# A fused transformer layer on one core: the cross attention's norm and query projection move behind the first experts, its query's copies to the end of the queue

## What is computed

```
x = x + norm(attn_block(norm(x)))
x = x + norm(moe_block(norm(x)))
attn_block(h): q,k,v = ln1(h) @ c_attn        # 16 heads of 8, causal
               h = h + softmax(q k^T) v @ attn_proj
               q = lnx(h) @ q_attn            # k,v from the encoder states
               h = h + softmax(q k^T + scorer, masked) v @ x_proj
               return h + gelu(ln2(h) @ fc) @ mlp_proj
moe_block(z):  shared swiglu expert + top 2 of 8 routed swiglu experts
```

## Time and profile before

| | before |
|---|---|
| median of three runs | 1736.7 us |
| the profiled execution | 1737.61 us |
| its span, first to last instruction | 1735.8 us |
| mean granted TensorE clock | 0.952 |
| TensorE busy | 1440.2 us, 83% |
| VectorE busy | 1122.1 us, 65% |
| ScalarE busy | 981.4 us, 57% |
| POOL busy | 314.1 us, 18% |
| DMA queue of SyncE (q1) | 54.43 MB, 17.9% of 16 engines' span |

### The profile page before, as it was taken

One profiled execution on the slowest core, in us unless ns is written; L12 is line 12 of the kernel. 1 busy time (PEld: TensorE's weight loads), 2 busy tenths in 40 slices (PEclk: granted clock), 3 DMA queues, 4 the chain that ended last, 5 costly groups with the idle time before them and its releaser, 6 DMA issues. The chain is left out here.

```text
span 1735.8 us, 39012 instructions
## 1 busy us (share of the span) xinstructions
PE 1440.2 (83%) x15448; PEld 888.5 (51%) x15448; DVE 1122.1 (65%) x3238; ACT 981.4 (57%) x1585; POOL 314.1 (18%) x426
## 2 busy tenths in 40 slices
PE   0186988899889898898889898988988898989867
PEld 0154656464655555464655555464655555555433
DVE  5146766676776767676766767776767767646334
ACT  0142566575665757574765757474756756471632
POOL 4102112121111212121211212121211112010110
PEclk9766889999999999999999999999999999998988
DMA  3121230402122130403122130303022121000000
GB/s 83 49 40 29 41 69 3 69 9 48 24 42 36 25 51 10 68 9 53 19 41 36 30 47 15 62 9 62 16 40 32 35 36 22 13 20 13 14 7 7
DMA packets 79214, 58.05 MB, mean 33 GB/s; under 512 B 11004, under 2 KB 78902, under 8 KB 79030
## 3 DMA queue, kind: packets, MB, share of 16 engines
q1 hardware_dynamic: 76084, 54.43, 17.9%
q10 hardware_dynamic: 2946, 1.12, 0.3%
HBM read 11.57 MB, written 4.19 MB: 9 GB/s over the span
## 5 line engine op out<-in xcount | busy, mean ns | idle before, releaser
L855 DVE TENSOR_REDUCE chunkmax<-ps 128x3 f32<-128x384 f32 (+1 forms) x1024 | 507.0, 553 | 110.0 <-PE ps L1139 104.8
L635 ACT ACTIVATE probs<-ps 128x768 f32<-128x768 f32 (+1 forms) x512 | 403.9, 809 | 134.9 <-PE ps L1134 130.8
L1202 PE MATMUL ps<-zT,w 128*128 128x512 f32 x576 | 277.6, 600 | 2.5 <-ACT silu_a L652 2.5
L652 ACT ACTIVATE silu_a<-ps,b 128x512 f32<-128x512 f32 x144 | 98.8, 686 | 200.5 <-PE ps L1202 200.3
L1119 PE MATMUL ps<-k_op,q_op 48*128 48x256 bf16 x512 | 149.6, 294 | 62.6 <-DVE chunkmax L855 45.4
L976 DVE SCALAR_TENSOR_TENSOR h_open<-ps,b,silu_a 128x512 f32<-128x512 f32 x128 | 95.9, 749 | 121.0 <-PE ps L1202 117.7
L1101 PE MATMUL ps<-q_op,k_op 51*128 51x256 bf16 x512 | 138.2, 279 | 39.5 <-ACT probs L635 18.3
L1202 PEld LDWEIGHTS ps<-zT,w 128*128 128x128 f32 x576 | 105.0, 191 | 111.0 <-issue 97.3
L1228 PE MATMUL ps<-hT,w 128*128 128x512 f32 x288 | 149.0, 598 | 12.4 <-DVE hT L982 12.4
L1131 PE MATMUL ps<-mask_q_lo,ident_lo 64*128 64x256 bf16 x512 | 149.0, 293 | 0.0
L1119 PE MATMUL ps<-xk_op,xq_op 51*128 51x256 bf16 x512 | 144.8, 284 | 5.0 <-DVE chunkmax L855 4.4
(11 more groups left out here) (232 smaller groups left out, 3425.4 us busy)
## 6 DMA issues: line engine op xcount, KB each, us to landing
q_op<-q_parts SPq DMA_DIRECT2D x192, 64.0 KB
k_op<-k_parts SPq DMA_DIRECT2D x192, 64.0 KB
xq_op<-xq_parts SPq DMA_DIRECT2D x192, 64.0 KB
x_tm<-in_L_attn_hidden_states SPq DMA_DIRECT2D x16, 256.0 KB, 6.0
x_keep<-in_L_attn_hidden_states SPq DMA_DIRECT2D x16, 256.0 KB, 6.1
out<-o_tm SPq DMA_DIRECT2D x16, 256.0 KB, 2.3
w<-in_L_ffn_rw SPq DMA_DIRECT2D x1, 1024.0 KB
q_op<-maxT SPq DMA_DIRECT2D x32, 24.0 KB
```

The lines of the kernel that those rows point to most:

```text
L635: act.activation(probs[:, four % 2, 2 * pair:2 * pair + 2, 0:T + a.seen], ps[:, 2 * (g % 2):2 * (g % 2) + 2, 0:T + a.seen], ACT.Exp).then_ ...
L652: act.activation(silu_a[:], ps[:, 0, :], ACT.Silu, bias=b1[:, e, 0:1]).then_inc(silu.sem, 1)
L855: dve.tensor_reduce(chunkmax[:, b, at, :], ps[:, MAX_BANK[n], 0:3 * a.seen].rearrange("p (c n) -> p c n", c=3), AX.X, ALU.max).then_inc(a. ...
L1202: pe.matmul(ps[:, bank, :], w, src[:], start=True, stop=True).then_inc(sig.sem, 1)
```

## The change

For pair i, the norm of the cross attention's input leaves the cross phase on VectorE, POOL and ScalarE. Its transposes on TensorE move from ahead of the router to behind the shared expert's down projection, and the matmul with `wxq` to between expert 2 and the context's transposes. ScalarE and VectorE take up the split of that query behind expert 1 and 2. On SyncE the DMAs of `xq_op` go behind those of `q_op` and `k_op`, and on POOL the low part goes behind theirs. The semaphore waits follow the banks that are now used in another order. No instruction is added or taken away. The diff, without a few lines of waits on TensorE:

```diff
@@ sync: body
-                if exists(i):
-                    operand(ca, q_rows, xq_parts, QPARTS, ca.qhi, ca.qmid, ca.qlo, ca.q_dma, i, par)
                 if exists(i + 2):
                     operand(sa, q_rows, q_parts, QPARTS, sa.qhi, sa.qmid, sa.qlo, sa.q_dma, i + 2, par)
                     operand(sa, k_rows, k_parts, KPARTS, sa.khi, sa.kmid, sa.klo, sa.k_dma, i + 2, par)
+                if exists(i):
+                    operand(ca, q_rows, xq_parts, QPARTS, ca.qhi, ca.qmid, ca.qlo, ca.q_dma, i, par)
@@ gpsimd: body
-                if exists(i):
-                    rstd(ca, tiny2, i)
...
                 if exists(i):
-                    low_part(xqr, xq_parts, ca.qr, ca.qmid, ca.qlo, ca.q_dma, i)
-
+                    rstd(ca, tiny2, i)
                     add_bias(h1b, h1, bxo, sa.h.done(i), ca.h.before(i), h1b_ready)
                 if exists(i + 2):
                     low_part(qr, q_parts, sa.qr, sa.qmid, sa.qlo, sa.q_dma, i + 2)
                     low_part(kr, k_parts, sa.kr, sa.kmid, sa.klo, sa.k_dma, i + 2)
+                if exists(i):
+                    low_part(xqr, xq_parts, ca.qr, ca.qmid, ca.qlo, ca.q_dma, i)
@@ scalar: body
                     exps(ca, i - 1, used, 4, 8)
-                if exists(i):
-                    act.wait_ge(*ca.xT_ps.before(i))
-                    normalise(ca, x2_tm, h1, (tiny2[:, 1, :], tiny2[:, 3, :]), ca.x_ready, i)
...
                     copy_out(ps[:, 0, :], zT[:], zT_ps.done(i - 2), b_ps.before(i - 2), zT_sb)
-                if exists(i):
-                    copy_out(ps[:, 2, :], xT[:], ca.xT_ps.done(i), sa.v_ps.before(i + 2), ca.xT_sb,
-                             cols[:, BX:BX + 1], cols[:, GX:GX + 1])
...
-                if exists(i):
-                    high_part(3, xqf, xq_parts, cols[:, BXQS:BXQS + 1], SCALE, ca.q_ps, ca.qr, ca.q_dma, ca.qf, ca.qhi, i)
...
                     values(i + 2, par)
+                if exists(i):
+                    act.wait_ge(*ca.xT_ps.before(i))
+                    normalise(ca, x2_tm, h1, (tiny2[:, 1, :], tiny2[:, 3, :]), ca.x_ready, i)
...
-                    experts(i - 2, 1, 3)
+                    experts(i - 2, 1, 2)
+                if exists(i):
+                    copy_out(ps[:, 2, :], xT[:], ca.xT_ps.done(i), sa.v_ps.before(i + 3), ca.xT_sb,
+                             cols[:, BX:BX + 1], cols[:, GX:GX + 1])
+                if exists(i - 2):
+                    experts(i - 2, 2, 3)
                 if exists(i - 1):
                     copy_out(ps[:, 6, :], ctxT[:], ca.nT_ps.done(i - 1), sa.o_ps.before(i), ca.nT_sb, cols[:, BXV:BXV + 1])
+                if exists(i):
+                    high_part(3, xqf, xq_parts, cols[:, BXQS:BXQS + 1], SCALE, ca.q_ps, ca.qr, ca.q_dma, ca.qf, ca.qhi, i)
@@ vector: body
                     maxima(sa, i + 1, 0, 6)
-                if exists(i):
-                    norm_stats(ca, h1, sa.h.done(i), st2, mv2, tiny2, i)
...
                     maxima_parts(sa, i + 1)
+                if exists(i):
+                    norm_stats(ca, h1, sa.h.done(i), st2, mv2, tiny2, i)
...
                     split_gates(k)
-                if exists(i):
-                    residual_parts(xqf, xqr, xq_parts, ca.qf, ca.qhi, ca.qr, ca.qmid, ca.qlo.before(i), i)
...
-                    for n in range(2, 5):
-                        products(k, n)
+                    products(k, 2)
+                if exists(i):
+                    residual_parts(xqf, xqr, xq_parts, ca.qf, ca.qhi, ca.qr, ca.qmid, ca.qlo.before(i), i)
+                if exists(k):
+                    products(k, 3)
+                    products(k, 4)
@@ tensor: body
                     transposes(ps[:, 0, :], z_tm, zT_ps)
-                if exists(i):
-                    pe.wait_ge(*ca.x_ready.done(i))
-                    transposes(ps[:, 2, :], x2_tm, ca.xT_ps)
...
                     max_rows(sa, 6, i + 1)
-                if exists(i):
-                    pe.wait_ge(*ca.xT_sb.done(i))
-                    by_feature(3, wxq[:], xT, ca.q_ps)
...
                     down(k, 0)
+                if exists(i):
+                    pe.wait_ge(*ca.x_ready.done(i))
...
+                    transposes(ps[:, 2, :], x2_tm, ca.xT_ps)
+                if exists(k):
                     experts(k, 2, 3)
+                if exists(i):
+                    pe.wait_ge(*ca.xT_sb.done(i))
+                    by_feature(3, wxq[:], xT, ca.q_ps)
```

More of the change, by code:

```diff
@@ L727, in body @@
                     act.activation(prob[:], logit[:], ACT.Exp).then_inc(gate_exp.sem, 1)
-                if exists(i):
-                    high_part(3, xqf, xq_parts, cols[:, BXQS:BXQS + 1], SCALE, ca.q_ps, ca.qr, ca.q_dma, ca.qf, ca.qhi, i)
                 if exists(i + 2):
-                    copy_out(ps[:, 2, :], xT[:], sa.xT_ps.done(i + 2), ca.q_ps.before(i + 1), sa.xT_sb,
+                    copy_out(ps[:, 2, :], xT[:], sa.xT_ps.done(i + 2), ca.q_ps.before(i), sa.xT_sb,
                              cols[:, B1:B1 + 1], cols[:, G1:G1 + 1])
@@ L1355, in body @@
                         pe.wait_ge(*sa.khi.done(i + 2))
-                    elif exists(i):
-                        pe.wait_ge(*ca.qhi.done(i))
                     context_T(ca, i - 1)
```

9 lines of the change are left out of this document (5 added, 4 removed).

## The result

The changed kernel takes 1995.84 us (median of 4 runs, 1992.14 to 2002.25) against 1736.86 us (4 runs, 1735.65 to 1737.61): a ratio of 1.1493, 95% interval 1.1473 to 1.1514. It is 259 us slower, where the forecast was 233.

The account below looks back on a forecast made before the run. TensorE's own work plus some 10 us of short gaps was taken to bound the 97.0 us iteration. Copies +220, cross phase -9, zT +8 and clock +14 give +233 us: 1970.6 from the profiled 1737.6, range 1899 to 2007.

Parts of the forecast that it names:

- The mechanism: SyncE and POOL: ca.h releases h1b, then q's low part; 26 DMAs follow before the self phase, the large term.
- The wait: TensorE ahead of the self phase, iterations 2 to 13: waits 14.6 us each for xq_op, 175 us.
- The start: Iterations 0 and 1: xq_op behind the other copies without experts as cover, 20 and 24.5 us lost.
- Iterations 14 and 15: No pair i+2: only two xq_op DMAs come after ca.h, in before the self phase; nothing lost.
- The cross phase: VectorE's statistics and ScalarE's x2 rows leave the scores: 0.55 us gained x 16, 9 us; bounds 0 to 1.47.
- The cover of zT's wait: Between the phases, TensorE's wait for zT's copy loses four transposes as cover: 0.6 us x 14, 8 us lost.
- The clock behind the wait: Self phase after the wait runs partly at TensorE's low clock: 1 us each, 14 us lost.
- Issue-paced transfers: Rival: SyncE's stream goes at the issue rate, 0.65 us a DMA, a wait of 10.4 us; 1913 us, chance 0.13.
- The hidden wait: Rival: h1b released by a DMA, not ca.h, so the experts cover the stream; 1729 us, chance 0.01 (level 0.01).
- The dear case: Rival: streams at 0.86 us a DMA, waits of 15.6 us, low clock 2 us each; 2007 us, chance 0.07.
- the small terms: Parts of the cross phase (x 16), zT (x 14) and clock (x 14) terms lying outside iterations 2 to 13.

Follow-up runs that it names:

- e1: The kernel before with only SyncE's order changed, q_op and k_op ahead of xq_op: 1991.64 us, ratio 1.147.
- e4: The changed kernel, SyncE's order kept, with h1b behind all three low parts on POOL: 1833.91 us, ratio 1.0561.
- e6: The changed kernel with xq_op between q_op and k_op on SyncE, its low part between theirs on POOL: 1847.89 us, ratio 1.0643.
- e3: The changed kernel with xq_op first again on SyncE and its low part ahead of h1b on POOL; computation stays moved: 1776.99 us, ratio 1.0226.
- e8: e7 with each moved block at its new place only where pairs i-2, i and i+2 all exist, elsewhere at its old one: 1748.22 us, ratio 1.006.
- e10: e8 with four unread matmuls per moved iteration in three TensorE waits between the phases: 1736.03 us, ratio 0.998.
- e9: The changed kernel with 18 unread matmuls in the wait ahead of each waiting self phase: 1980.65 us, ratio 1.1396.
- e11: Control: the kernel before with the last three of e10's four unread matmuls: 1739.63 us, ratio 1.0005.
- e5: The changed kernel with 15 unread matmuls in the wait ahead of each waiting self phase: 1987.06 us, ratio 1.1427.
- e2: The kernel before with only POOL's order changed, xq's low part behind h1b and q's and k's low parts: 1748.22 us, ratio 1.0067.
- e7: e3 with q_op's ten early DMAs ahead of xq_op on SyncE and its two of the low part behind: 1768.68 us, ratio 1.0176.

## Why the prediction was right, step by step

- **The mechanism.** Right at each link: `ca.h` releases `h1b` (the row now names it), POOL holds q's low part, the queue holds 26 DMAs behind that, and TensorE waits for the last of them. e1 shows that SyncE's order is the cause, e4 that q's low part has to stand behind `h1b` for it, and e6 that the number of DMAs sets the size.
- **The wait, forecast 14.6 us x 12 = 175.** Measured 15.3 on average and 15.9 typically, 183. From q's low part (831.87) to the landing near 857.0 are 25.1 us and not 23.9, by the forecast's fixed 2.8 us a pace of (25.1 - 2.8)/26 = 0.86 us for each, not 0.81. The windows show 82 GB/s at the stream's start and 92 over the wait, so the DMAs move no less than forecast, but not for the stream alone. The forecast left out the input loads of 256 KB each that SyncE issues right behind `xq_op`, while it is still under way. Iteration 13 has one of them in place of two. From q's low part to TensorE's start (windows), then the loads (SyncE), in the iteration shown and in iteration 13:

```profile
831.87:857.12 25.25, 8.59 (x22) 3.29 (x21) 6.31 (x18) 2.06 (x3) 3.45 (x5) 0.73 0.60 85
1637.32:1659.33 22.01, 8.59 (x21) 3.28 (x20) 6.30 (x18) 2.06 (x3) 3.45 (x5) 0.76 0.53 90
...
848.90 0.39 SPq L374 DMA_DIRECT2D x_tm<-in_L_attn_hidden_states  x1
849.34 0.54 SPq L380 DMA_DIRECT2D x_keep<-in_L_attn_hidden_states  x1
...
1654.83 0.45 SPq L380 DMA_DIRECT2D x_keep<-in_L_attn_hidden_states  x1
```

The stream's 26 x 65,536 bytes are 1.70 MB; the first window moved 2.15 MB, the second 1.98. With less beside it the stream was in after 22.0 us, by the fixed 2.8 us 0.74 for each DMA, and e1 has the same (22.1 us). So the loads are a part of the slower pace. They are not all of it: iterations 2, 7 and 8 have both loads and need 23.5 to 23.8 us. The Trainium skill (DMA: Bandwidth & Descriptors, Anatomy of one DMA), whose figures gave an estimated wait of 9.1 us, does not agree with this trace, which has 15.3.
- **The start, forecast +20 and +24.5.** Measured +21.9 and +25.2. In iteration 0 the 36 DMAs run from 161.28 to TensorE's start at 194.91, 0.86 us for each, and in iteration 1 the 26 need 25.4 us; both have the same slightly slower pace.
- **Iterations 14 and 15, forecast nothing.** Measured +3.8 and +2.4. There is indeed no new wait of size for `xq_op`; in 14 the self phase (+2.4) and the stretch behind the cross phase (+1.2) are longer. In 15 it is the stretch from the cross phase to `h`, 22.10 before and 24.90 after. In both, TensorE waits 1.9 us for VectorE's `gate_parts` there, where it waited 0.64 before, and in 15 the clock is 0.93 on the stretch's mean and was 1.00. These iterations have no query, key and value of a pair i+2 any more. That the move has a price where this work is missing was not in the sum. e3 shows the same (+1.8, +2.6).
- **The cross phase, forecast -0.55 us x 16.** At full clock the cross phase takes 23.85 in place of 24.96, a gain of 1.1 us, twice the forecast and within its bounds. But in nine of the twelve iterations the clock falls within the phase (0.93 on its mean), and it takes 25.1 to 25.2 us; before the change a low stretch there, in six of twelve, cost some 0.25 us. So 0.25 us a phase are left (3 us over twelve).
- **The cover of zT's wait, forecast 0.6 us x 14.** The wait grew from 0.31 to 0.75 us, by 0.44. The stretch it lies in is 26.70 in place of 26.26, and 26.86 on the mean. What the forecast missed is a second effect: where the clock falls in this stretch it costs 1.7 us more, once in the changed kernel but often in e3 and e8. That this wait, with the others near it, helps to bring the clock down is argued from e10, which filled three of them together; no run filled it alone.
- **The clock behind the wait, forecast 1 us x 14.** Low for 7 to 10 us and not 4; self phases take 1.7 us more on average, 2.4 where it lasts 10 us. e9, which takes 1.5 of the 1.7 us away, shows that this is the low clock's doing. Per us of low clock that is under a quarter. VectorE's maxima (5%) and ScalarE's exponentials (4%) are on the chain too, which may be the reason. Charging half of the low time, as the Trainium skill (TensorE: Matmul & The Clock Gate, HAM oscillation) would, gives 5 us for 10, and these phases don't show it.
- **The rivals.** Issue-paced transfers (1913) are out: 0.86 us a DMA, 0.74 at the least, not 0.65. The hidden wait, the faster side, is out: POOL starts 0.15 us behind VectorE's `h`. The dear case (2007) had the pace right, 0.86 us, and the clock nearly (2 us for 1.7), but left the cross phase's gain out; the result lies between it and the forecast. That the pace came out so is no merit of its reasoning, which did not name the input loads.

Summed, measured less forecast: the wait +8, the clock in iterations 2 to 13 +8 (20 for 12), the last two iterations and the end +5, the cross phase +4 (a gain of 3 for 12 x 0.55 = 6.6), the start +2.5, zT's stretch 0 (7 for 12 x 0.6), and -1 for the small terms that the forecast had outside of these iterations. That is +27, and the profiled executions differ by 260 where the forecast had 233: the large terms are near. Two small ones are near by luck, since they hold two errors that cancel: the cross phase (a larger gain, less low clock) and zT's stretch (a smaller wait, plus low clock). **What stays open** is what besides the input loads sets the pace (0.74 to 0.86 us), what brings the low stretches left in e10, and a proof that the stops in e3 are instruction loads.

## What to carry to other kernels

An in-order DMA queue passes a wait on: before a block of copies is put behind others, ask what the last part of those others waits for and on which engine, then count every DMA between that point and the one that is needed; here 26 DMAs at 0.86 us outran 9 us of cover. Count also what is issued right behind: with one input load fewer there the stream was in 1.5 to 3 us sooner. That a block can be moved for a gain (0.7 us an iteration here) is worth little until the copies it feeds keep their place, its first and last iterations keep theirs, and the waits that it used to fill are filled. Look at the granted clock by stage after such a move, since where short waits stood together it fell, and filling them brought most of it back.

## What the runs showed of the hardware that was not expected

- Twelve DMAs of 64 KB are issued by SyncE in 7.8 us, 0.65 each, but 26 in a row land at about 0.86 us each, in the changed kernel as in e1, with two input loads of 256 KB behind them, and at 0.74 us each with one (iteration 13 of both).
- Gaps of 0.75 to 1.2 us that stand near each other were in most iterations, not in all, followed by 3.4 us at half clock, at a price of 1.2 to 1.7 us (e3, e8). Unread matmuls in them removed most of it (e10: 96.14 us at clock 1.00), and in the kernel before, which loses only some 0.25 us to such stretches, they cost nothing (e11, 1.0005).
- A wait of 16 us that is filled except for its last 2.8 us was followed by 7 to 10 us of low clock all the same (e5); filled to the last 0.45 us, by 3.4 us of it in most phases, which then took 22.85 us and not 22.21 (e9).
- TensorE stopped for 3.3 and 3.4 us with no wait that the profile shows, the first time while DMAs moved 95 to 100 GB/s (e3), and once for 1.28 us (e2). Each time it went on 1.5 to 1.6 us after a 16 KB load of the instruction queue had ended. Nothing like it was seen where the stream was issued 6 us earlier against the phase (e7). That is strong evidence for late instruction loads, not proof.
